# Handing out the attention work of the next block in pieces between the matmul groups of the mixture of experts

## What is computed

```python
x_sh = pad(x)[:, :-1, :]                      # x, one position earlier
key   = x*tmk + x_sh*(1-tmk);  value = ...;  receptance = sigmoid(...)
k = key @ Wk.T;  v = value @ Wv.T;  r = receptance @ Wr.T      # 1024 x 1024
# per channel, position after position:
q = max(u+k_t, w); e1 = exp(-w-q); e2 = exp(u+k_t-q)
a = e1*a + e2*v_t; b = e1*b + e2;  wkv_t = a/b
x = layernorm(x + (wkv*r) @ Wo.T + bo)
logits = x @ Wr.T + br                        # 8 experts, top 2, softmax
h = relu(einsum('bsd,efd->bsef', x, W1) + b1) # 8 experts, 1024 -> 4096
o = einsum('bsef,edf->bsed', h, W2) + b2      # 4096 -> 1024
tgt2 = sum over e of o[e]*router_w[e]
x = layernorm(x + layernorm(x + tgt2)*gamma + beta)
```

## Time and profile before

| | us |
|---|---|
| timed runs, median of 2 | 11730.81 |
| the two timed runs | 11452.75 and 12008.88 |
| the profiled execution | 11343.23 |
| its span, slowest core (core 3) | 11341.4 |
| its span, fastest core (core 5) | 11289.5 |

### The profile page before, as it was taken

One profiled execution on the slowest core, in us unless ns is written; L12 is line 12 of the kernel. 1 busy time (PEld: TensorE's weight loads), 2 busy tenths in 40 slices (PEclk: granted clock), 3 DMA queues, 4 the chain that ended last, 5 costly groups with the idle time before them and its releaser, 6 DMA issues.

```text
span 11341.4 us, 107902 instructions; the slowest of 8 cores (11289.5 to 11341.4 us)
## 1 busy us (share of the span) xinstructions
PE 8690.3 (77%) x42240; PEld 4040.2 (36%) x42240; DVE 1556.5 (14%) x3542; ACT 2366.3 (21%) x3362; POOL 1413.6 (12%) x1232
## 2 busy tenths in 40 slices
PE   3565556557888688867888688867888688868997
PEld 3222222224444344434444344434443344434443
DVE  5010010112111211122111211122111211121001
ACT  1111111112222222222222222222222222222222
POOL 0111111110111011110111011110111011110111
PEclk7777877768999899988999799988999799988998
DMA  3555555443333233323333233323333233323443
GB/s 68 118 122 124 125 121 133 117 100 102 121 121 119 89 123 123 120 93 102 121 121 118 88 123 121 123 95 102 121 121 117 86 122 121 123 96 110 138 137 105
DMA packets 326769, 1290.80 MB, mean 114 GB/s; under 512 B 29625, under 2 KB 95418, under 8 KB 251074
## 3 DMA queue, kind: packets, MB, share of 16 engines
q1 hardware_dynamic: 296962, 1124.51, 29.4%
q0 software_dynamic: 29312, 159.40, 8.0%
HBM read 1275.40 MB, written 153.09 MB: 126 GB/s over the span
## 4 chain that ended last, share of the span: by engine, by line
PE 49%; DMA 30%; DVE 11%; ACT 4%; issue 3%; POOL 1%; another core or an unknown queue 1%; SPq 0%; DVEq 0%; POOLq 0%; ACTq 0%
DMA arena<-w2C 13%; PE psB L680 7%; PE psA L680 7%; PE psC L680 7%; PE psD L680 7%; DMA arena<-w2H 6%; PE psB L711 5%; PE psA L711 4%; PE psD L711 4%; DMA arena<-w1H 4%; PE psC L711 4%; DMA w2C<-arena 3%; DMA w1C<-arena 2%; DMA xch<-xH 1%; PE psA L465 1%
## 5 line engine op out<-in xcount | busy, mean ns | idle before, releaser
L728 POOL TENSOR_TENSOR otmp<-otmp,rwbc 128x512 f32<-128x512 f32 x512 | 646.6, 1263 | 7344.1 <-ACT otmp L724 7284.2
L680 PE MATMUL psA<-x1bf,arena 128*128 128x512 bf16 x4096 | 1096.3, 416 | 418.3 <-DMA arena<-w1H 226.0
L711 PE MATMUL psB<-arena 128*128 128x512 bf16 x4096 | 997.8, 402 | 251.1 <-DMA arena<-w2H 131.1
L711 PE MATMUL psA<-arena 128*128 128x512 bf16 x4096 | 976.2, 396 | 233.1 <-DMA arena<-w2H 113.5
L711 PE MATMUL psD<-arena 128*128 128x512 bf16 x4096 | 966.6, 394 | 180.6 <-DMA arena<-w2H 105.5
L711 PE MATMUL psC<-arena 128*128 128x512 bf16 x4096 | 954.6, 391 | 187.5 <-DMA arena<-w2H 139.6
L680 PE MATMUL psB<-x1bf,arena 128*128 128x512 bf16 x4096 | 1027.5, 396 | 58.2 <-POOL tgt L736 56.1
L299 DVE TENSOR_TENSOR arena<-xch 128x1024 f32<-128x1024 f32 x32 | 47.1, 1472 | 6868.9 <-ACT xch L295 6868.9
L680 PE MATMUL psC<-x1bf,arena 128*128 128x512 bf16 x4096 | 974.9, 381 | 0.0
L680 PE MATMUL psD<-x1bf,arena 128*128 128x512 bf16 x4096 | 967.6, 379 | 0.0
L680 PEld LDWEIGHTS psA<-x1bf,arena 128*128 128x128 bf16 x4096 | 418.0, 104 | 986.9 <-issue 587.9
(11 more groups left out here) (143 smaller groups left out, 5012.3 us busy)
## 6 DMA issues: line engine op xcount, KB each, us to landing
arena<-w1C SPq DMA_DIRECT2D x448, 1024.0 KB, 5.6
arena<-w2C SPq DMA_DIRECT2D x896, 512.0 KB, 3.8
arena<-w1H POOLq DMA_DIRECT2D x64, 1024.0 KB, 8.7
w1C<-arena SPq DMA_DIRECT2D x64, 1024.0 KB, 4.1
arena<-w2H POOLq DMA_DIRECT2D x128, 512.0 KB, 5.5
w2C<-arena SPq DMA_DIRECT2D x128, 512.0 KB, 2.7
xch<-xH SPq DMA_DIRECT2D x32, 512.0 KB, 7.2
arena<-woC POOLq DMA_DIRECT2D x8, 2048.0 KB, 12.6
```

What stands on the lines that cost most here:

```text
L680: grp = p.op("tensor", lambda e, jd=jd, fc=fc, buf=buf, bk=bk: e.matmul(bank[bk][:, 0:TQ], w1s[buf][:, jd, fc * 128:(fc + 1) * 128], x1bf. ...
L711: grp = p.op("tensor", lambda e, jf=jf, jfi=jfi, buf=buf, bk=bk: e.matmul(bank[bk][:, 0:TQ], w2s[buf][:, jfi, :], hsb[:, jf, :], start=(jf ...
L728: t_om = p.op("gpsimd", lambda e: e.tensor_mul(otmp[:], otmp[:], rwbc[:]), waits=[t_oc, t_rwbc], inc="gpsimd")
```

## The change

`seg` becomes a generator, `seg_gen`, with 15 `yield` statements that cut a chunk's work into 16 pieces; the statements themselves and their waits are unchanged. A list `pending` holds the generator, and `pump(n)` emits its next n pieces (2 unless told otherwise):

```diff
+        pending = []
 
         def seg(q, c):
+            g = seg_gen(q, c)
+            for _ in g:
+                pass
+
+        def pump(n=2):
+            k = 0
+            while pending and k < n:
+                try:
+                    next(pending[0])
+                    k += 1
+                except StopIteration:
+                    pending.pop(0)
+
+        def seg_gen(q, c):
...
                     nxt = (e_, s_ + 1) if s_ + 1 < 8 else ((e_ + 1, 0) if e_ + 1 < E else None)
                     if nxt is not None:
                         ensure_w1(q, nxt[0], nxt[1], t_w1dma, w1_buf_of)
+                    pump()
...
                         ensure_w2(q, e_ + 1, 0, t_w2dma, w2_buf_of)
+                    pump()
                     t_oc = p.op("scalar", lambda e, bk=bk, e_=e_, dc=dc: e.activation(
...
                 t_rwbc_prev = t_tg
                 if e_ % 2 == 0 and q + 1 < NQ:
-                    seg(q + 1, e_ // 2)
+                    pending.append(seg_gen(q + 1, e_ // 2))
+                pump(6)
+            while pending:
+                pump(100)
```

More of the change, by code:

```diff
@@ L301, in seg @@
                 waits=[t_c0, ("gwc", 0)] + gate, inc="vector")
+            yield
             t_mk = t_mv = t_mr = None
```

## The result

The changed kernel is faster: the comparison with the kernel before gives a ratio of 0.970, 95% interval 0.966 to 0.975. Its profiled execution takes 11103.3 us (11343.2 before, forecast 11,100). The median of all its timed runs is 11695.6 us, outside the range of 11,050 to 11,500; that of the kernel before, over more runs now, is 11960.7. In most executions of either kernel the cores of one or both dies show a lower granted clock (0.76 to 0.88 as a mean) and take up to 10% longer, so the medians of all runs are far above the profiled executions, and the ratio is taken from the two lowest timed runs on each side (11103.3 and 11115.3 against 11444.1 and 11452.8).

The account below looks back on a forecast made before the run. PE, busy in 77% of the span, was taken to set the time, its waits being lost. Savings of 217 us (blocks 1 to 6) plus 28 (block 0), 245 in all, take 11343 to 11098, say 11,100; range 11,050 to 11,500.

Parts of the forecast that it names:

- The stop of psA goes with ACT's order: Inside FFN1, psA's 28 waits for ACT's eviction, 191.5 us, vanish once eight ACT instructions move behind slabs 1, 2, 4.
- 9.52 or 7.85 us a place, 217 us for blocks 1 to 6: Standing plus slow matmuls saved at FFN1's stop: 17 places at 9.55 us and 7 at 7.85.
- Nothing is late next, with 1.7 us to spare: ACT's longest moved portion, behind slab 2 of FFN1, takes 3.6 us of 5.3 free between evictions; costed at nothing.
- Block 0: 28 us: Block 0's W1 load chain starts sooner with R behind slab 0: 7.0 us at each of 4 places, between 0 and 38.
- K's and V's waits stay: Ahead of FFN1, PE's waits for the mixed x (230.9 us) and K's evictions (165.3 us) remain unchanged.
- The range, 11,050 to 11,500: Whole kernel's measured time in us; upper end is the old median less 245, slower runs left out.
- The third rival: Whole chip: less clock is granted as PE works more densely; 11,654 us with a slow run behind the change; chance 0.03.
- the range given for the forecast itself, 11,060 to 11,150: Whole kernel in us: blocks 1 to 6 save between 188 and 235, block 0 between 0 and 38.
- the first rival: Only part comes back, within 2% (227 us): block 0's gain lost (11,126) or slow matmuls anyway (11,149); chance 0.32.

Follow-up runs that it names:

- r_only: Against the changed kernel, only R's matmuls and the step reading them go behind slab 0, all other chunk work back ahead of FFN1: 11360.9 us.
- again: The changed kernel unaltered, timed anew beside the kernel before: medians 11,610 against 12,077 us; medians of runs at full clock give a ratio of 0.980.
- late2: Against the changed kernel, pieces handed out earlier and wider: x load and mixing inside the even expert's FFN2, K behind it, V behind slab 0: 10651.4 us.
- late: Against the changed kernel, all pieces stand inside FFN1 of the odd expert, x load behind slab 0 to R behind slab 4: 10679.4 us.
- the execution with two copies: The changed kernel with two more 128x1024 copies on ACT behind the first exponential, in the portion behind slab 2: 11356.4 us, one die's clock lowered.

## Why the prediction was right in its mechanism and wrong in its range

**The stop of psA goes with ACT's order.** Right. All 28 waits are gone, and `r_only` shows that it is this and not the move of R.

**9.52 or 7.85 us a place, 217 us for blocks 1 to 6.** Right. From V's last matmul to FFN1's last a place now takes 58.7 us at 137 of 144 places (six cores) and at most 59.6, 9.1 us less as a mean than before, where the stride gives 32 groups of 1.73 us and R's 3.57. In the chain of waits the router's matmuls of blocks 1 and 7 begin at 2579.87 and 10020.96 us, 1240.2 us a block in place of 1278.3 (2594.57 to 10264.43): 229 us. That this is so close to 217 is in part luck. Ahead of V the places take 0.5 us more than before (24.5 us from FFN2's last matmul to V's last, now 25.0), which takes back 12 us. FFN2's waits for its weights are 27 us shorter (on the profiled cores 293.6 us in place of 320.9, from the groups by line), and that is scatter: in `again`, the same kernel, FFN2 takes as long as before, and a block there takes 1240.0 us as a mean over six cores, 1237.2 in the first execution, 1275.8 in the kernel before.

**Nothing is late next, with 1.7 us to spare.** Right, and measured: 0.28 us of waiting at 5.7 us, 2.54 at 8. The table load took 1.28 us and the exponential followed 0.01 us behind it, with ACT busy right up to the load. The Trainium skill (ScalarE: Activation LUTs, section "What ACT_TABLE_LOAD costs") gives 2.66 us for a switch, with a drain beside the load; between an eviction and an exponential this trace doesn't agree.

**Block 0: 28 us.** Mis-sized. The step was 7.0 us a place; it measured 5.4 (131.1 to 125.7), 22 us over the four. The first load does come 3.57 us sooner, and the next follows in a chain's length, but that length was 13.75 us here and 13.0 in the row I used, and what came sooner by more than R's move was only 1.5 us. Even these 22 us aren't kept: from the first matmul of FFN1 in block 0 to that in block 1 it is 2309.4 us before (mean over six cores), 2295.1 in the changed kernel's first execution and 2307.6 in `again`, so 14 and 2 us less. The forecast had named this as its lower bound, that a later wait takes it back; which wait does stays open.

**K's and V's waits stay.** Right, and this was the larger part: the forecast costed them as untouched and didn't ask what they would give. `late2` took another 466 us by them (11,117 to 10,651; 24 × 17.7 = 425 us at the places of blocks 1 to 6).

**The range, 11,050 to 11,500.** This is where the prediction failed: measured 11695.6. The step was "I take 11,500, the old median less 245, and leave runs beyond it out". It took the median of two runs, 11730.8, for that of the program. Ten runs of it have 11960.7, and 11960.7 − 245 = 11,716 is within 0.2% of what was measured. The two runs shown were 5% apart, and the wider statement was to be had from them: with one of two runs at 12,009, that most runs lie there could not be excluded, and the range had to go up to 12,009 − 245 = 11,764. The third rival had even worked out such a run, at 11,654 with a chance of 0.03, and the range stopped below it. Such runs need no change of the kernel: they are most of the runs of either. Beside this, the range given for the forecast itself, 11,060 to 11,150, is added up wrongly: 11,343 less 235 and 38 is 11,070, and 11,343 less 188 is 11,155.

**The third rival, that the change itself costs clock.** Nothing of it is seen. Of 36 dies in 18 runs of the kernel before 19 were under 0.883; of 40 in 20 runs of the changed kernel 21 were under 0.889. The lowered clock comes about as often to the one as to the other. For the still denser `late2` and `late` ten dies of 16 were lowered, too few to tell. What I had said against the Trainium skill's rule beside it, that all cores were busy at 1.00, rests on something that the rows don't show; see the last section.

**Chances.** Faster by over 2% had 0.62. The comparison says 3.0%, the runs at full clock 2.0 to 2.2%, so the closeness to 2% was rightly seen. At full clock the change is worth 228 us (11,345 to 11,117), between the forecast's 245 and the 217 of the first rival's case in which block 0's gain is lost.

## What to carry to other kernels

An instruction that another engine needs soon must not stand behind a chain that the same engine works through in turns with a third: count how many groups the banks hold, and hand the chain out in portions. A portion between two evictions is free up to the pause between them plus the slack of the banks (1.04 + 4.2 us here), and one experiment that lengthens it tells whether that margin is real. When one of several waits at the same place is taken away, ask of the others what the same means would bring; here they held twice as much.

When the timed runs that one has lie 5% apart, the forecast of a mechanism and the forecast of a median are two things, and the range must hold the second.

## What the runs showed of the hardware

A third level of the granted clock beside 0.5 and 1.0, which no row of the kernel before had. In the execution with two copies, core 2, FFN1 runs like this near the end of the span:

```profile
10750.33 2.27 PE L713 MATMUL psC<-x1bf,arena 128*128 128x512 bf16 x8
10752.42 2.28 PE L713 MATMUL psD<-x1bf,arena 128*128 128x512 bf16 x8
```

2.10 us from group to group in place of 1.73, a factor of 1.21, with PE busy throughout. A window over 100 us of it:

```profile
10750.00:10850.00 100.00, 97.64 (x358) 39.57 (x364) 0.00 (x0) 17.76 (x26) 15.18 (x12) 0.80 0.35 116
```

The clock's records there read 0.81, which is between the two levels; on core 2 they add up to 1488 us of this span.

All four cores of die 0 have such stretches, and no core of die 1. But they lie at different places of the program: on cores 0 and 1 between 79 and 1940 us, on cores 2 and 3 between 9442 and 11299 us. Windows of core 0:

```profile
300.00:1900.00 1600.00, 1029.95 (x3592) 404.12 (x3593) 103.22 (x276) 201.87 (x298) 189.56 (x229) 0.70 0.54 123
...
9500.00:11000.00 1500.00, 1299.56 (x6215) 593.39 (x6216) 128.52 (x282) 359.87 (x511) 202.89 (x161) 0.94 0.37 122
```

and of core 2:

```profile
300.00:1900.00 1600.00, 957.11 (x3541) 390.89 (x3605) 102.58 (x272) 201.95 (x299) 192.54 (x232) 0.78 0.53 124
...
9500.00:11000.00 1500.00, 1338.33 (x5430) 578.76 (x5524) 128.49 (x282) 311.69 (x440) 192.72 (x153) 0.79 0.33 109
```
